# Score products from fp32r values and remainders, stacked in TensorE's row groups, in a fused attention and mixture-of-experts kernel

## The reference

```python
# attention: 32 query heads, 8 key heads, 16 features each; the context is key and value
q = layernorm(x); k = v = ctx                      # x (32, 128, 512), ctx (32, 128, 128)
scores = einsum('bkgsd,bktd->bkgst', qh, kh) / 4   # 4 query heads share a key head
out = einsum('bkgst,bktd->bkgsd', softmax(scores), vh)
x = x + tanh(g_xattn) * out
# experts: 8, top 2
z = layernorm(x)
logits = tanh(z @ Wg1.T) @ Wg2.T
scores = softmax of the 2 highest, 0 elsewhere
down = silu(z @ Wup.T + bup) @ Wdown.T + bdown     # per expert, 256 hidden features
x = x + tanh(g_ffn) * sum over experts of scores * down
```

## Time and profile before

| | |
|---|---|
| median of 3 runs | 698.03 us (696.45 to 698.19) |
| the profiled execution, time | 695.72 us |
| its span, first to last instruction | 693.9 us |
| busy: TensorE, its weight loads | 91%, 62% of the span |
| busy: VectorE, ScalarE, GpSimd | 75%, 55%, 51% |
| chain of work that ended last | TensorE 77%, VectorE 11%, issue 4%, DMA 2%, GpSimd 2% |
| granted TensorE clock, mean | 0.978 of full |

### The profile page before, as it was taken

The page is one execution under the profiler, slowest core; times in us unless marked ns, Lnnn a source line. Parts: engine busy times, 40 slices in busy tenths (PEclk is TensorE's granted clock), DMA queues, the critical chain, the costliest instruction groups (busy, mean ns, idle before and its releaser), DMA issues.

```text
span 693.9 us, 17038 instructions
## 1 busy us (share of the span) xinstructions
PE 634.2 (91%) x5064; PEld 432.1 (62%) x5064; DVE 521.6 (75%) x1456; ACT 378.3 (55%) x692; POOL 353.8 (51%) x538
## 2 busy tenths in 40 slices
PE   3779999999999999999999977899999999999970
PEld 2435555555555555555555466789998888888850
DVE  3468888888888888888888455476767788887763
ACT  2267777777767676767676531333334544544430
POOL 4123545464545455656665536890032666575454
PEclk9999999999999999999999989899999999999995
DMA  3123344444444444444432677344665999999977
GB/s 103 53 66 116 114 141 149 139 142 141 144 140 144 140 144 141 145 141 145 143 126 77 208 279 256 109 154 152 215 227 177 304 348 345 348 354 352 334 250 256
DMA packets 65032, 129.40 MB, mean 186 GB/s; under 512 B 8640, under 2 KB 12736, under 8 KB 64704
## 3 DMA queue, kind: packets, MB, share of 16 engines
q1 hardware_dynamic: 44496, 77.35, 32.9%
q0 software_dynamic: 10368, 33.56, 14.3%
q10 hardware_dynamic: 10096, 17.59, 7.8%
HBM read 74.20 MB, written 54.26 MB: 185 GB/s over the span
## 4 chain that ended last, share of the span: by engine, by line
PE 77%; DVE 11%; issue 4%; DMA 2%; POOL 2%; ACT 1%; SPq 1%; DVEq 0%; ACTq 0%; POOLq 0%
PE s_ps L1281 13%; PE bank_a L1260 8%; PE st_ps L1304 8%; DVE nmax L993 7%; PE st_ps L1398 5%; PE st_ps L1399 5%; PE st_ps L1400 5%; PE s_ps L1379 4%; PE bank_c L1221 3%; PE bank_b L1269 3%; PE st_ps L1312 3%; PE bank_q L1356 2%; PE bank_a L1411 2%; PE bank_a L1412 2%; PE bank_a L1410 2%
## 5 line engine op out<-in xcount | busy, mean ns | idle before, releaser
L993 DVE TENSOR_REDUCE nmax<-s_ps 128x8 f32<-128x1024 f32 x128 | 156.4, 1222 | 62.3 <-PE s_ps L1281 61.2
L754 ACT ACTIVATE probs<-st_ps 128x1024 f32<-128x1024 f32 x128 | 131.2, 1025 | 67.2 <-PE st_ps L1312 63.6
L1281 PE MATMUL s_ps<-k_t,q_t 32*128 32x256 f32 x1024 | 151.9, 415 | 17.2 <-DVE nmax L993 14.4
L1304 PE MATMUL st_ps<-q_t,k_t 32*128 32x512 f32 x512 | 145.6, 645 | 0.3
L1281 PEld LDWEIGHTS s_ps<-k_t,q_t 32*128 32x128 f32 x1024 | 92.6, 192 | 68.9 <-DVE nmax L993 44.7
L695 POOL DMA_INDIRECT y<-expert_out,rows_all x64 | 64.6, 1009 | 57.7 <-DMA expert_out<-y_sb 43.3
L1398 PE MATMUL st_ps<-w_hi,zh 128*128 x284 | 86.9, 306 | 1.3 <-DVE zl L1092 1.3
L1399 PE MATMUL st_ps<-w_lo,zh 128*128 x284 | 80.7, 284 | 0.0
L1400 PE MATMUL st_ps<-w_hi,zl 128*128 x284 | 80.5, 283 | 0.0
L831 ACT ACTIVATE t_sb<-u_sb 128x256 f32<-128x256 f32 x71 | 29.7, 418 | 87.1 <-DVE u_sb L1102 78.1
L656 POOL DMA_INDIRECT slots<-z,slot_i x64 | 64.6, 1009 | 16.0 <-issue 15.7
(11 more groups left out here) (182 smaller groups left out, 1376.6 us busy)
## 6 DMA issues: line engine op xcount, KB each, us to landing
expert_out<-y_sb SPq DMA_DIRECT2D x71, 256.0 KB, 3.9
z_s<-slots ACTq DMA_DIRECT2D x67, 256.0 KB, 3.9
x_in<-in_x SPq DMA_DIRECT2D x32, 256.0 KB, 2.7
wst<-in_w SPq DMA_DIRECT2D x32, 256.0 KB, 2.6
x_res<-in_x SPq DMA_DIRECT2D x32, 256.0 KB, 2.8
x_scratch<-x_res SPq DMA_DIRECT2D x32, 256.0 KB, 2.0
r_in<-x_scratch SPq DMA_DIRECT2D x32, 256.0 KB, 5.4
out<-r_in SPq DMA_DIRECT2D x32, 256.0 KB, 5.1
```

What stands on the lines that cost most here:

```text
L754: a.activation(out, st_ps[:, :].rearrange("t (k n) -> t k n", k=2), ACT.Exp, scale=HD ** -0.5).then_inc(exp_done[half], 1)
L993: v.tensor_reduce(out, s_ps[:, :].rearrange("s (r g c t) -> s r g c t", r=2, g=2, c=2), X_AXIS, ALU.max, negate=True).then_inc(max_done, 1)
L1281: last = t_.matmul(s_ps[:, HALF * rr + 2 * P * gg:HALF * rr + 2 * P * (gg + 1)], q_t[r2][row:row + ROWS32, P * g_:P * (g_ + 1)], k_t[r2][r ...
L1304: t_.matmul(st_ps[:, HALF * rr:HALF * (rr + 1)], k_t[r][row:row + ROWS32, P * i:P * (i + 1)], q_t[r][row:row + ROWS32, :], start=True, sto ...
```

## The change

The three fp32 operands of the score products become fp32r, each split in a value and a remainder.

- **Queries.** VectorE writes the normalization to `q_n` (the same memory as `z_t`). ScalarE copies it to fp32r, the value (`q_half(0)`), and VectorE subtracts that from `q_n`, the remainder (`q_half(1)`). Value and remainder of a head stand next to each other in `q_hl`, 32 columns per head, so that 32 rows of contraction now hold one head's value and remainder. TensorE brings them to `q_t` by eight products with an identity matrix in fp32r (`query_rows(0)` before `weighted_sum(1)`, `query_rows(1)` after it) instead of four transposes.
- **Keys.** ScalarE copies each key head twice to fp32r, GpSimd subtracts for the remainder; four products with the identity instead of one transpose, one ScalarE copy of 512 columns instead of two of 128 with `parity`.
- **Score block.** Eight score products per row group of 128 moving columns (`score(0)` to `score(7)`: 4 query and key heads, key value and key remainder) instead of two of 256 in fp32; `across(0)` and `across(1)` are the transposed products with key value and key remainder. `s_done` is raised by `score(7)`, now the last of the block.
- **Orders.** `weighted_sum` takes the heads of one `i`, so it waits for one exponential of each half. `v_aug` moves to after the second query copy.
- **Loops.** All 36 steps are written out.
- **Buffers.** `q_t`, `k_t`, `v_aug` in rings of 3 instead of 4, the mixing's `y1`, `y2` in rings of 4 instead of 3, and `dynamic_dma_scratch_size=8192` is given to the compiler.

```diff
-def pipeline(eng, step, steps, first, last, unroll):
+def pipeline(step, steps, unroll):
 
-    for s in range(first):
-        step(s, s % unroll)
-    with eng.Fori(0, (last - first) // unroll) as i:
-        for u in range(unroll):
-            step(i * unroll + (first + u), (first + u) % unroll)
-    for s in range(last, steps):
+    for s in range(steps):
         step(s, s % unroll)
...
+        def keys_twice(t):
+            return t[:, :].rearrange("p (k d) -> p k d", d=HD).unsqueeze(2).to_broadcast([P, KV, 2, HD])
+        def q_half(i):
+            return q_hl[:, :].rearrange("p (n i d) -> p n i d", i=2, d=HD)[:, :, i, :]
...
@@ SP, step
-                    wait(sp, kt_done, b - 1)
+                    wait(sp, k_lo_done, b - 1)
                     wait(sp, v_done, b - 1)
                     sp.dma_start(c_in[p][:, :], ctx_d[bass.ds(b, 1), :, :].rearrange("a s d -> (a s) d")).then_inc(c_loaded[p], 16)
...
@@ GpSimd, step
                 if valid(b1):
+                    pool.wait_ge(k_hi_done, b1 + 1)
+                    g.tensor_tensor(k_hl[:, 2 * P:4 * P].rearrange("p (k u d) -> p k u d", u=2, d=HD),
+                                    keys_twice(c_in[u1]),
+                                    k_hl[:, 0:2 * P].bitcast(F32).rearrange("p (k u d) -> p k u d", u=2, d=HD),
+                                    ALU.subtract).then_inc(k_lo_done, 1)
                     pool.wait_ge(w_hi_done, b1 + 1)
...
@@ ScalarE, step
+                def keys(b):
+                    act.wait_ge(kt_done, b + 1)
+                    wait(act, st_done[1], 2 * (b - TRING) + 2)
+                    a.activation(k_t[r1][:, :], bank_c[:, :], ACT.Copy).then_inc(kt_copied, 1)
+                def queries(b, c):
+                    act.wait_ge(qt_done, 2 * b + c + 1)
+                    a.activation(q_t[r1][:, c * D:(c + 1) * D], (bank_q, bank_c)[c][:, :],
+                                 ACT.Copy).then_inc(qt_copied, 1)
+                if valid(b1):
+                    act.wait_ge(c_loaded[p1_], ring2(b1, p1_))
+                    wait(act, kt_done, b1)
+                    a.activation(k_hl[:, 0:2 * P].rearrange("p (k u d) -> p k u d", u=2, d=HD),
+                                 keys_twice(c_in[p1_]), ACT.Copy).then_inc(k_hi_done, 1)
                 if valid(b4):
                     exps(b4, 1, 0)
...
                 if valid(b4):
                     exps(b4, 1, 1)
+                if valid(b1):
+                    act.wait_ge(n_done, b1 + 1)
+                    wait(act, qt_done, 2 * b1)
+                    a.activation(q_half(0), q_n[:, :].rearrange("p (n d) -> p n d", d=HD), ACT.Copy).then_inc(q_hi_done, 1)
+                if valid(b4):
                     o_out(b4, 0)
+                if valid(b3):
+                    exps(b3, 0, 0)
                 if valid(b1):
+                    keys(b1)
+                    queries(b1, 0)
+                if valid(b4):
+                    o_out(b4, 1)
+                if valid(b1):
+                    queries(b1, 1)
+                    wait(act, pv_done, 2 * (b1 - TRING) + 2)
                     a.activation(v_aug[r1][:, :].rearrange("p (k c) -> p k c", c=32)[:, :, 0:HD],
...
                 if valid(b3):
                     exps(b3, 0, 1)
                 if valid(b5):
+                    act.wait_ge(q_lo_done, b1 + 1 if valid(b1) else B)
                     gate_rows(b5)
...
@@ VectorE, step
                     dve.wait_ge(n_rs, b1 + 1)
-                    wait(dve, qt_done, b1)
-                    v.tensor_scalar(q_perm[:, :].rearrange("s (g k d) -> s k g d", g=G, d=HD),
+                    if valid(b6):
+                        dve.wait_ge(lg1_done, b6 + 1)
+                    v.tensor_scalar(q_n[:, :].rearrange("s (g k d) -> s k g d", g=G, d=HD),
...
                     logits(b6, p6_)
+                if valid(b1):
+                    dve.wait_ge(q_hi_done, b1 + 1)
+                    v.tensor_tensor(q_half(1), q_n[:, :].rearrange("p (n d) -> p n d", d=HD),
+                                    q_half(0).bitcast(F32), ALU.subtract).then_inc(q_lo_done, 1)
                 if valid(b2):
                     maxima(2)
...
@@ TensorE, step
+                def query_rows(c):
+                    for g_ in range(G):
+                        last = t_.matmul((bank_q, bank_c)[c][:, P * g_:P * g_ + P], heads_of(q_hl, g_, c),
+                                         ident_r[:, :], start=True, stop=True)
+                    last.then_inc(qt_done, 1)
...
-                    def part(gg):
+                    def score(n):
+                        gg, c, part_ = n // 4, n // 2 % 2, n % 2
+                        g_ = 2 * i + gg
                         for rr in range(2):
-                            row, g_ = ROWS32 * (2 * half + rr), 2 * i + gg
-                            last = t_.matmul(s_ps[:, HALF * rr + 2 * P * gg:HALF * rr + 2 * P * (gg + 1)],
-                                             q_t[r2][row:row + ROWS32, P * g_:P * (g_ + 1)],
-                                             k_t[r2][row:row + ROWS32, :], start=True, stop=True,
-                                             tile_position=(row, 0))
+                            row, at = ROWS32 * (2 * half + rr), HALF * rr + P * (2 * gg + c)
+                            last = t_.matmul(s_ps[:, at:at + P],
+                                             q_t[r2][row:row + ROWS32, c * D + P * g_:c * D + P * (g_ + 1)],
+                                             k_t[r2][row:row + ROWS32, (2 * part_ + c) * P:(2 * part_ + c + 1) * P],
+                                             start=(part_ == 0), stop=(part_ == 1), tile_position=(row, 0))
                         return last
...
                     if valid(b2):
-                        part(1).then_inc(s_done, 1)
+                        for n in range(1, 4):
+                            score(n)
+                    if valid(b):
+                        across(1)
+                    if valid(b2):
+                        for n in range(4, 7):
+                            score(n)
                     if valid(b):
...
                         last.then_inc(st_done[over], 1)
+                    if valid(b2):
+                        score(7).then_inc(s_done, 1)
...
                     rows_back(b4, 0)
-                    weighted_sum(b4, r4, 1)
                 if valid(b1):
-                    pe.wait_ge(c_loaded[p1_], ring2(b1, p1_))
+                    pe.wait_ge(k_lo_done, b1 + 1)
...
-                    t_.transpose(bank_c[:, 0:P], c_in[p1_][:, :], ident_f[:, :]).then_inc(kt_done, 1)
+                    for n in range(4):
+                        last = t_.matmul(bank_c[:, P * n:P * n + P], heads_of(k_hl, n // 2, n % 2), ident_r[:, :],
+                                         start=True, stop=True)
+                    last.then_inc(kt_done, 1)
...
+                    pe.wait_ge(q_lo_done, b1 + 1)
+                    query_rows(0)
+                if valid(b4):
+                    weighted_sum(b4, r4, 1)
+                if valid(b1):
+                    pe.wait_ge(kt_copied, b1 + 1)
+                    query_rows(1)
                 scores(3)
```

More of the change, by code:

```diff
@@ L176, in block_kernel @@
         z_t = sb("z_t", [P, D], F32, p1)
+        q_n = z_t
         tooth = sb("tooth", [P, PAIRS], F32, p1)
@@ L425, in _ @@
             g.memset(tick[:, :], 1.0).then_inc(const_ready, 1)
-            for i in range(RING):
+            for i in range(TRING):
                 g.memset(v_aug[i][:, :], 0.0).then_inc(const_ready, 1)
@@ L448, in _ @@
             last = g.memset(v_aug[0][:, :].rearrange("p (k c) -> p k c", c=32)[:, :, HD:HD + 1], 1.0)
-            for i in range(1, RING):
+            for i in range(1, TRING):
                 last = g.memset(v_aug[i][:, :].rearrange("p (k c) -> p k c", c=32)[:, :, HD:HD + 1], 1.0)
@@ L1301, in scores @@
                             pe.wait_ge(nmt_copied, b + 1)
[L1302 to L1308 removed]
+                        across(0)
+                    if valid(b2):
+                        for n in range(1, 4):
[5 more added lines that the diff above has]
+                            score(n)
                     if valid(b):
@@ L1353, in step @@
                     elif valid(b2):
-                        pe.wait_ge(qt_copied, b2 + 1)
-                    for g_ in range(G):
-                        last = t_.transpose(bank_q[:, P * g_:P * g_ + P], q_perm[:, P * g_:P * g_ + P], ident_f[:, :])
-                    last.then_inc(qt_done, 1)
+                        pe.wait_ge(qt_copied, 2 * b2 + 1)
+                    pe.wait_ge(q_lo_done, b1 + 1)
[5 more added lines that the diff above has]
+                    query_rows(1)
                 scores(3)
```

121 lines of the change are left out of this document (58 added, 63 removed).

## The result

| | before | after |
|---|---|---|
| median | 697.24 us (695.3 to 698.19, 4 runs) | 725.98 us (723.64 to 732.67, 4 runs) |
| ratio | | 1.0436, 95% interval 1.0391 to 1.0481 |
| profiled execution, span | 695.72, 693.9 us | 723.64, 721.9 us |
| first maximum of scores starts at | 12.0 us | 14.6 us |
| the next five steps, together | 60.3 us | 66.6 us |

Slower, by 28.0 us of span. It is lost up to the last maximum 0: 2.6 before the first maximum, 6.3 in the next five steps, 23.2 in the 26 steps behind them; the tail of attention gives back 3.0 and the second part 1.1.

The account below looks back on a forecast made before the run. Bound: VectorE from block 3 to block 1, TensorE in the rest of the 11.52 us step. 27 steps x 0.6 = 16.2, +2 ramp, -2 unrolling, -1.5 tail: +14.7, forecast 712 us (case 705 to 723, overall 696 to 728).

Parts of the forecast that it names:

- tail: Last three attention steps, without score products: other products shrink by 0.42 per block, -1.5 us (0 to -3).
- second part: Experts and mixing after attention: otherwise the same despite four y tiles and a given DMA scratch size, 0 (-1 to +1).
- product's price: One fp32r product of 128 columns with its weight load on TensorE: 0.109 us, between 0.053 and 0.24.
- query and key groups: TensorE, between rows_back(0) and block 3: twelve products for five transposes, 1.37 us for 0.70, +0.67 per step.
- item 3: ScalarE copies the queries' value ahead of o_sb: rows_back(0) starts 4.05 us after block 1, TensorE waiting 0.55.
- VectorE's remainder: VectorE's subtraction for the queries, between logits and maximum 2: about 0.6 us, covered, cost 0; uncovered 0.6 per step.
- unrolling: The attention loop written out: gain 2 us (0 to 3).
- streaming price: Rival: products at 0.053 to 0.06 us, extra key and query products free, 688 to 693 us, faster; chance 0.14.
- slow fp32r: Rival: fp32r products of 128 columns take 0.2 us or more, blocks of 2 us, some 850 us; chance 0.03.
- hidden copy: Rival: the value copy ahead of o_sb is hidden, step about 11.8 us, 703 us in all; chance 0.12.
- item 6: Keys' value copy on ScalarE and remainder on GpSimd: fit into idle time or are needed later, cost 0.
- ramp: Four partial steps at the start, with a longer chain from x to the first block: +2 us.

Follow-up runs that it names:

- e6: Changed kernel with three of the four products of the second query group left out: 714.2 us in one run.
- e1: Changed kernel with ScalarE's value copy of the queries moved behind the copy of weighted sum 0 to o_sb: 726.28 us, ratio 1.0365.
- e5: Changed kernel with normalization right after maximum 0, an earlier value copy, and GpSimd's key and weight remainders moved later: 715.03 us, ratio 1.0231.
- e3: Changed kernel with VectorE's remainder of the queries left out but for one head of 32: 730.84 us, ratio 1.0421.
- e4: Kernel before with steps 12 to 23 written out instead of the loop, nothing else: 694.34 us, ratio 0.9959.
- e9: Changed kernel with GpSimd subtracting the keys' remainder for only 16 of its 256 columns: 723.81 us, ratio 1.0375.
- e2: Changed kernel with GpSimd's key remainder moved from ahead of w_lo to behind the residual sum: 731.91 us, ratio 1.0439.
- e12: The kernel of e5 with the added unread products of e11: 716.78 us, ratio 1.0295.
- e11: Changed kernel with unread products: 14 before TensorE's first work, 4 before the first score block, 3 behind each block of steps 2 and 3: 728.42 us.
- e10: The kernel of e4 with the unread products of e7 at the start: 692.04 us, beside 696.03 for the kernel before.
- e7: Changed kernel with unread products: 7 before TensorE's first work, 3 behind each score block of steps 2 and 3: 739.75 us, ratio 1.0588.

## Why the prediction was right in sign and short by half

The forecast was 712 (+14.7), the result 726 (+28.0 in the profiled execution), above the 705 to 723 of the forecast.

**Right.** The product's price (0.109 forecast, 0.11 in e6) and with it the query and key groups: rows_back(0) to block 3 took 2.99, forecast 2.95. The score block, 1.03 for 1.0, and its small use: block 3 to block 1 took 5.15, forecast 5.17, because VectorE sets that stretch. The new wait in ScalarE's queue, with its releaser (item 3; e1 and e5 take it away and gain). VectorE's remainder at no cost (e3). The unrolling, 2 forecast, 1.9 to 2.3 measured (e4). The tail gave 3.0, the end of its bounds, and the second part 1.1, just past its own.

The streaming price fell with 0.11 per product; its opponent, the 190 ns of the earlier trace rows, is now 197 in the products' own row. The rule of the Trainium skill quoted there (TensorE: Matmul & The Clock Gate, "Weight-path perf modes": fast load for 128 weights that are not FP32) shows no effect on these fp32r products. The slow fp32r, with blocks of 2 us, fell as well: blocks of 1.97 exist, but at the lower clock, where everything else is twice as long too. The hidden copy fell with the 0.39 before rows_back(0).

**Wrong: item 6, "GpSimd ... Cost 0", and through it the size of item 3.** The prediction asked which engines wait for GpSimd's results, and nothing else. GpSimd's work also holds up two of VectorE's operations that run at the same time: the mask sum takes 0.97 instead of 0.27, the normalization 0.65 instead of 0.54, both between block 1 and the value copy, on the very path of item 3. The 0.7 of the mask sum is mostly hidden by the wait for the scores that stood there before (0.59 in the earlier trace rows): maximum 1 comes 0.08 later than forecast, and with the normalization's 0.11 that is 0.19. Block 1 to rows_back(0) became 4.33 instead of 4.05; e9 gives 4.12 without the key remainder. The other 0.07 lies behind the copy: from o_sb's start to rows_back(0) it is 0.73 here (0.65 forecast); the value copy held ScalarE 0.53 (0.50 forecast). The Trainium skill (SBUF — State Buffer, "Who interferes with whom") says that a VectorE instruction with two inputs in SBUF and a GpSimd instruction that reads SBUF exclude each other, and that the first to start holds the other up for its whole length. The trace agrees: the mask sum has two such inputs, starts 0.34 after w_lo and ends 0.04 behind it, in e9 0.02 behind it, in the kernel before 0.03. That sentence speaks of two inputs; the normalization reads one tensor, and that it is held up too is what e2 and e9 show (0.72 beside the key remainder, 0.54 with nothing beside it).

Item 3 also had TensorE free for rows_back(0) at 3.5. It was free at 3.94, since block 2 stands behind the mask sum as well, so its wait was 0.39 instead of 0.55.

A step costs 0.95 more instead of 0.6. The 26 steps behind the first five took 324.5 us against 299.5 in e4: 25.0 instead of the 16.2 of the sum, 8.8 of the 13.3 missing. By e9 the key remainder is 0.2 per step, some 5.2 of the 8.8. Another 0.1 per step, some 2.6, are the hand-overs and the copy above and the 2.99 for 2.95. The rest is mostly the sum itself: its terms, 7.00 and 5.17, make 12.17, were written as 12.15 and entered as 12.1. (Two more slips, which do not move the forecast: the rival of the hidden copy, 6.30 - 0.5 + 0.67 + 5.17, is 11.64 and not 11.8, and 698.0 + 14.7 is 712.7.)

**Wrong: the ramp, "+2".** It cost 9.4 against e4 (2.6 to the first maximum, 66.6 against 59.8 in the next five steps): 7.4 of the 13.3. (The tail and the second part gave 2.6 more than forecast and the unrolling 0.3, which closes the sum.) The forecast counted the longer chain from x to the first block, not TensorE's clock. Across the traced executions of kernels without added products, the first five steps follow the time from which the matmuls stay fast (the clock record that ends the slow stretch):

| kernel | fast from (us) | first five steps (us) |
|---|---|---|
| e4 | 33.7 | 59.8 |
| after | 49.0 | 66.6 |
| e9 | 51.2 | 67.3 |
| e1 | 68.8 | 72.5 |
| e3 | 83.2 | 78.9 |
| e2 | 84.2 | 78.9 |
| e5 (fast from 49.2 to 56.0 too) | 93.6 | 79.9 |

For e2, e3 and e5 the traced execution is the longest of the four.

From after to e3 that is 12.3 us for 34.2, 0.36 per us. At this rate a rise at 33.7 would give 66.6 - 15.3 x 0.36 = 61.1, near e4: an estimate by which about 5.5 of the 9.4 is the clock's. The clock also sets apart single executions of one kernel where its records reach back to the start: the mean granted clocks of e12, 0.960, 0.943, 0.943 and 0.931, go with 707.37, 716.72, 716.84 and 721.42 us, those of e11, 0.957, 0.956, 0.947 and 0.935, with 724.88, 725.14, 731.7 and 736.78. In e11 the longest execution was (1 - 0.935) x 734.9 / 0.5 = 96 us at half clock and the shortest (1 - 0.957) x 723.0 / 0.5 = 62: 11.9 us for 33 to 34, again about 0.36 per us. That the same explains the 9 to 15 us between the executions of after, e2 and e3 isn't shown: their records begin too late, and the kernel before has spreads of 3 us (the four beside after) and of 9 (the thirteen beside e1 to e4).

What e10 and e11 show, in one traced execution each, is that idle time at the start isn't enough to explain the late clock: with it filled, the fp32r kernel loses the clock and the fp32 kernel doesn't. The two slower executions of e10 were not traced. That the fp32r products are the cause is the nearest reading, not shown by itself: whether it is the score blocks or the key and query groups was not separated, and why the rise differs so much between kernels that differ by one moved instruction stays open.

The lowest medians are those of the kernel before with its loop written out (694.34 against 697.73), and of the same with products at its start (692.04, from executions of 686 to 698).

## What to carry to other kernels

Before an operation is booked at no cost on an idle engine, look not only at who waits for its result, but at what runs beside it: here 0.72 us on GpSimd cost VectorE 0.8 in two short operations, and each step 0.2. The sign in a trace is a short VectorE operation that ends just behind a GpSimd operation. Shortening a block pays only in the stretch where that block sets the pace; write the step as a sum of start distances, as here, and each stretch can be checked against the trace by itself. And price the first steps apart from the regular ones: here they ran at another clock.

## What the hardware showed unexpectedly

- An addition of 128x8 elements on VectorE took 0.10 us alone (e5) and 0.27, 0.45 or 0.97 (before, e9, after), by how long a GpSimd subtraction that had started before it still had to run: it ended 0.02 to 0.04 behind it each time.
- TensorE at half clock (0.50 granted) for 28 us and for 68 us while busy 97% of the time, with score products of 128 columns in 32 rows (e11, e7); the same matmuls at full clock later, at 87% (e11, 50 to 90 us).
- Products that nobody reads, at the start, made the first steps of the fp32 kernel 5.6 us shorter (e10) and those of the fp32r kernel longer (83.3 against 66.6 in e7, 68.1 in e11), in one traced execution each.
